# Step zero of a fused attention and mixture-of-experts kernel: weights loaded in halves, VectorE's first work in another order, state copies on ScalarE

## What is computed

```python
q, k, v = xn @ Wq, (xn @ Wk) * DK ** (-0.5), xn @ Wv      # 8 heads, DK = 128, DV = 64
alpha = sigmoid((xn @ Wg + bg) / 16)                       # one per token and head
state = alpha_t * state + k_t[:, None] * v_t[None, :]      # token after token
out_t = q_t @ state
att = (out * sigmoid(xn @ Wog)) @ Wo
```

## Time and profile before

| | us |
|---|---|
| median of 3 runs | 1261.15 (1260.3 to 1261.98) |
| the profiled execution | 1266.82 |
| its span, as the profile shows it | 1265.1 |
| busy in the span: PE | 1237.9 (98%) |
| DVE | 976.6 (77%) |
| ACT | 624.3 (49%) |
| POOL | 487.4 (39%) |

### The profile page before, as it was taken

The page is one execution under the profiler, slowest core; times in us unless marked ns, Lnnn a source line. Parts: engine busy times, 40 slices in busy tenths (PEclk is TensorE's granted clock), DMA queues, the critical chain, the costliest instruction groups (busy, mean ns, idle before and its releaser), DMA issues.

```text
span 1265.1 us, 28662 instructions
## 1 busy us (share of the span) xinstructions
PE 1237.9 (98%) x9910; PEld 1092.2 (86%) x9910; DVE 976.6 (77%) x2343; ACT 624.3 (49%) x1319; POOL 487.4 (39%) x377
## 2 busy tenths in 40 slices
PE   7899999999999999999999999999999999999999
PEld 6788888887888888799899998989989999889987
DVE  6997878889797659878688687786885877868844
ACT  6675756666574544344444444444444444434432
POOL 2110111011001027237467385474574754845620
PEclk9999999999999999999999999999999999999999
DMA  6576534354352322357486575674774765748665
GB/s 241 170 250 200 188 110 156 122 190 158 121 171 60 111 75 84 95 145 186 105 198 165 130 178 136 150 181 106 188 171 121 172 155 137 193 104 191 162 194 183
DMA packets 124920, 194.68 MB, mean 154 GB/s; under 512 B 12016, under 2 KB 98608, under 8 KB 124592
## 3 DMA queue, kind: packets, MB, share of 16 engines
q1 hardware_dynamic: 94384, 147.99, 36.1%
q0 software_dynamic: 30464, 45.83, 19.7%
HBM read 148.62 MB, written 57.74 MB: 163 GB/s over the span
## 4 chain that ended last, share of the span: by engine, by line
PE 76%; DVE 16%; issue 5%; ACT 2%; another core or an unknown queue 0%; DVEq 0%; DMA 0%; ACTq 0%
PE bank L793 21%; PE bank L808 7%; PE bank L905 7%; PE bank L937 7%; PE bank L845 6%; PE bank L825 5%; PE bank L877 3%; PE bank L863 3%; PE bank L866 3%; PE bank L948 3%; PE bank L836 3%; DVE Dt L1506 3%; PE bank L889 2%; PE bank L927 2%; DVE At L1527 2%
## 5 line engine op out<-in xcount | busy, mean ns | idle before, releaser
L635 POOL DMA_INDIRECT acc<-arena,idx_all x128 | 224.3, 1752 | 149.4 <-DMA acc<-res 54.1
L627 POOL DMA_INDIRECT arena<-table,idx_all x132 | 163.6, 1240 | 153.8 <-ACT share L1160 96.5
L793 PE MATMUL bank<-xp,wq 128*128 128x512 f32 x768 | 208.4, 406 | 0.0
L793 PE MATMUL bank<-xp,wk 128*128 128x512 f32 x768 | 202.2, 398 | 0.0
L793 PEld LDWEIGHTS bank<-xp,wk 128*128 128x128 f32 x768 | 138.5, 188 | 29.3 <-DVE wk L1416 0.4
L793 PEld LDWEIGHTS bank<-xp,wq 128*128 128x128 f32 x768 | 136.6, 189 | 25.4 <-issue 0.8
L1506 DVE TENSOR_TENSOR_SCAN Dt<-decay,eye_b 128x512 f32<-128x512 f32 x128 | 157.7, 1233 | 0.0
L845 PE MATMUL bank<-qT,kT 128*128 128x128 f32 x1024 | 136.2, 275 | 1.8 <-DVE At L1527 1.4
L1136 ACT ACTIVATE kT<-bank 128x512 f32<-128x512 f32 x128 | 76.7, 599 | 118.0 <-PE bank L793 102.2
L845 PEld LDWEIGHTS bank<-qT,kT 128*128 128x128 f32 x1024 | 125.2, 192 | 3.3 <-DVE At L1527 1.6
L1136 ACT ACTIVATE qT<-bank 128x512 f32<-128x512 f32 x128 | 76.9, 601 | 85.4 <-PE bank L793 64.7
(11 more groups left out here) (174 smaller groups left out, 2317.1 us busy)
## 6 DMA issues: line engine op xcount, KB each, us to landing
decay<-decay_dram SPq DMA_DIRECT2D x64, 512.0 KB
carry<-decay_dram SPq DMA_DIRECT2D x60, 512.0 KB
arena<-in_L_attn_x_dram SPq DMA_DIRECT2D x16, 512.0 KB, 4.5
table<-arena SPq DMA_DIRECT2D x16, 512.0 KB, 3.2
xT_dram<-arena SPq DMA_DIRECT2D x16, 512.0 KB, 3.0
arena<-in_L_ffn_w_gate_dram SPq DMA_DIRECT2D x64, 128.0 KB
arena<-in_L_ffn_w_up_dram SPq DMA_DIRECT2D x64, 128.0 KB
arena<-in_L_ffn_w_down_dram SPq DMA_DIRECT2D x64, 128.0 KB
```

The source lines that it names most:

```text
L627: pool.indirect_dma_start(out=xg[:, e % 2, j, :], out_offset=None, in_=table[:, :], in_offset=bass.IndirectOffsetOnAxis(ap=idx_all[:, e, j ...
L635: pool.indirect_dma_start(out=acc[:, :], out_offset=bass.IndirectOffsetOnAxis(ap=idx_all[:, e, j:j + 1], axis=0), in_=yb[:, e % 2, j, :], ...
L793: last = mm(to[:, :], w[:, part, k, h * DK:(h + 1) * DK], xp[:, other, k, :], start=(k + i == 0), stop=(k == KD - 1 and i == 2))
```

## The change

Loading. The weights q and k are loaded in halves of four heads each (`q0`, `k0`, `q1`, `k1`), as are their splits. SP's order is x, Wv, gate_w, Wg, q0, k0, the two biases (on a semaphore of their own, `w_bias`), x of block 1 into a buffer of its own (`xt1`, the `addend` tile), og, q1, k1, o. PE waits for gate_w and Wg only.

PE. 24 identity transposes in place of 18 at the start and 6 more between `tokens_back(0, 1)` and `router(0)`; `router(0)` waits for DVE's copies of the tokens and no longer for ACT's; `decays_across(0)` stands behind the first q projection instead of ahead of it.

DVE, ahead of step 0. Splits `v` ahead of the tokens; `gates(0)` ahead of the q and k splits, which are halves; `statistics(1)` ahead of `route_groups(0)`; `route_ranks(0)` and `route_top(0)` ahead of step 0 with the first scans between them; two scans ahead of step 0, not four.

DVE, in step 0. A table of its own for the scans (`first_scans`), with the q1, k1 and o splits in s = 2, 3 and 5; the scan of head 3 of block 1 stands behind all of step 0. No state copies: they are ACT's, `state_first`, at s = 2, 4, 6 and 8 ahead of the high part of `gT`.

ACT, in step 0. `normalise(1)` and the token copies of block 1 (`tokens`) ahead of `keys_weighted(0, 0)`, which moves from ahead of s = 1 into it; the high parts of q1, k1 and o in s = 1, 2 and 3.

SP, in step 0. `norm_io(1)` ahead of `load_decay(0, 3)`.

The end. The third and the fourth pair of batches 0 and 1 are done together, batch after batch.

```diff
-PE_WARM = 18
+PE_WARM = (24, 6)
...
+        xt1 = addend[:, :, :]
...
             def step(c, kind, more=True):
                 first = isinstance(c, int) and c == 0
+                if first:
+                    norm_io(1, more=True)
                 load_decay(c, 3)
...
             tokens_back(0, 0)
             tokens_back(0, 1)
+            for _ in range(PE_WARM[1]):
+                tr(bank[5][:, 0:P], ident[:, :], ident[:, :])
             router(0)
...
                 proj_v(c, kind, 0)
                 if first:
-                    decays_across(0)
                     pe.wait_ge(w_split, 2)
                 proj_qk(c, kind, 0, 0)
+                if first:
+                    decays_across(0)
...
-            out_part(0, (2,))
-            out_part(1, (2,))
             for b in range(B):
-                out_part(b, (KO - 1,))
+                out_part(b, (2, KO - 1) if b < 2 else (KO - 1,))
...
+            def state_first(p):
+                act.wait_ge(u_ps, p + 1)
+                f(state[:, 2 * p:2 * p + 2], bank[6][:, :].rearrange("p (b u v) -> p u b v", b=B, u=2), ACT.Copy)\
+                    .then_inc(state_up, 1)
...
+                    if first and s < 4:
+                        weights_high(("q1", "k1", "o")[s - 1])
+                    if first and s % 2 == 0:
+                        state_first(s // 2 - 1)
                     if s % 2 == 0:
                         outs_high(c, s // 2 - 1)
...
-            tokens_low(0)
             weights_low("v")
-            dve.wait_ge(w_const, 64)
-            weights_low("q")
+            tokens_low(0)
+            dve.wait_ge(w_bias, 32)
             gates(0)
+            weights_low("q0")
+            weights_low("k0")
             decays_products(0)
-            weights_low("k")
+            statistics(1)
             route_groups(0)
-            statistics(1)
-            weights_low("og")
-            scales(1)
...
+            def first_scans(s):
+                for c, h in {1: ((0, 2),), 2: ((0, 3),), 3: ((0, 4),), 4: ((0, 5), (0, 6)), 5: ((0, 7), (1, 0)),
+                             7: ((1, 1), (1, 2)), 9: ((1, 3),)}.get(s, ()):
+                    decay_scan(c, h)
+                if s in (2, 3, 5):
+                    weights_low({2: "q1", 3: "k1", 5: "o"}[s])
...
+            weights_low("og")
+            scales(1)
+            route_ranks(0)
             decay_scan(0, 0)
+            route_top(0)
             decay_scan(0, 1)
-            weights_low("o")
-            decay_scan(0, 2)
-            decay_scan(0, 3)
             step(0, "norm")
```

93 lines of the change are left out of this document (59 added, 34 removed).

## The result

The changed kernel takes **1262.53 us** (median of 22 executions, 1259.92 to 1264.69), the kernel before beside it 1260.72 us (1260.20 to 1262.62, 22 executions): ratio 1.0013, 95% interval 1.0007 to 1.0019. By the forecast's bound of 0.2% this counts as unchanged; by the interval it is a little slower. Forecast were 1257.1 us, in a range that ended at 1261.0 us. The time lies above the range, and it moved in the other direction.

What follows compares the result with a forecast made beforehand. DVE was taken to bound step 0, PE the later steps. Terms -1.45 - 2.05 - 1.64 + 1.2 = -3.94 us, with -0.1 us for the end, took 1261.15 to 1257.1 us; range 1254.9 to 1261.0 us, 8 in 10.

Steps and rivals of the forecast that it cites:

- The start: Ahead of step 0: PE's clock rises early, DVE's copy of the transposed decays starts at 17.5 instead of 18.95 us, -1.45 us.
- Rival 1: At the start: PE's clock does not rise early, decays' copy comes about 20.9 us, total 1260.6 us; chance 0.28.
- The q and k loads: At the start: these loads land behind Wv alone instead of behind the small ones and Wv; costed at nothing.
- the other scans: DVE's step 0 stretch: other scans, o's split, ranks and choice are only reordered; nothing, while others wait for DVE.
- So step 0 costs what stands in DVE's list between those two points: Step 0: DVE's list from the decays' copy to the end of `tokens_low(1)`, 68.43 us, plus the start, sets its length.
- State copies: Step 0: three copies of 0.685 us ahead of `tokens_low(1)` go from DVE to ACT, -2.05 us.
- (a): Step 0, s = 4: DVE waits longer for `gT`'s high part because ACT makes a state copy first, +0.6 us.
- The scan behind: Step 0: the scan of head 3 of block 1 goes behind DVE's stretch, -1.64 us.
- (b): Step 0: DVE waits bare for ACT's square root in s = 6 and the router in s = 8; 0 to 2.8, taken +0.6 us.
- Behind step 0: Entry to step 1: moved scan and later transfers delay DVE against PE; up to 2 us without cover, taken as 0.
- The end: Last output parts and stores: reordered batches change the end by -0.3 to +0.1 us, taken as -0.1 us.
- Rival 2: Step 0: ACT's added copies and high parts make others wait, 1263.2 us; sign: PE waits for ACT over 4 us; chance 0.12.

Runs made afterwards that it cites:

- the second trace: Profiled execution of the unmodified changed kernel, run again on a calmer chip; PE starts step 1 at 86.47 us; that series measured 1261.74 us, ratio 1.0011.
- the short warm-up: Changed kernel with 18 identity transposes at the start and none between token transposes and router: 1263.57 us, ratio 1.0002.
- the new end alone: Kernel before with only the new order of the last output parts: 1261.43 us, ratio 1.0004.
- before with empty instructions: Kernel before with 16 empty instructions ahead of DVE's list, which the build leaves out: ratio 0.9998.
- late loads: Changed kernel with SP's loads of q1, k1 and o issued behind the first two loads of decays: 1263.16 us, ratio 0.9996.
- both edits: Changed kernel with late loads and ACT's square roots of blocks 2 and 3 behind the keys' eviction and update copy: 1262.51 us, ratio 0.9995.
- The combination: Changed kernel with both edits, the old order at the end, and ACT's state copy behind the outputs' high part: first measured 1258.79 us, ratio 0.9984.

## Why the prediction was wrong

The walk of the prediction, step by step:

- **The start, -1.45 us.** Right in mechanism and size: copy at 17.07 us (17.5 forecast; 17.49 us in the second trace). The term was worked out with the router at 1.90 us from 11.7 us on, so with a clock that has risen by then. That was the author's assumption: no row of before shows it that early (3.69 us at 12.37 us). The changed kernel does: nothing but transposes ran from 3.26 us, the eight of 8.89 us take 1.09 us in place of 1.97, and the router 2.00 us from 10.92 us. Rival 1, the late clock, is out. The forecast's premise, that 18 transposes do not bring the rise, was a chance of its trace, though: of the five traces with 18, three (the short warm-up, the new end alone, before with empty instructions) also show the eight in 1.09 to 1.10 us. What holds in all seventeen is the router, 3.69 us with 18 and 2.00 us with 24 and 6. But the gain was not to be had, see the next point.
- **"The q and k loads ... I cost them at nothing", and "the other scans ... only put in another order: nothing". The step that failed first.** The two transfers of decays were never costed, though the reordering puts the first scan behind them at an earlier time. SP has issued the same transfers ahead of the store of the decays, 32 KB, in both kernels (before it issues the second block at 19.45 us, 1.0 us ahead of that store), but the store now comes 1.9 us earlier, while SP is done with issuing the weights and the stores of block 0 3.0 us later (16.00 us against 13.02, the table's store alone taking 4.05 us in place of 0.39). From the store to the loads it is 6.2 us in place of 3.1. Price: 3.1 us of DVE (1.6 us in the second trace). The experiment with late loads gives it back: no wait, and 66.25 us of stretch, 66 forecast.
- **"So step 0 costs what stands in DVE's list between those two points", and PE starting step 1 "right behind" `tokens_low(1)`. Failed too.** With DVE's list shorter PE becomes the bound from s = 6 on: it starts step 1 1.15 us behind `tokens_low(1)` in the changed kernel, in both its traces and with late loads, without a wait. With late loads DVE is done at 83.43 us, as forecast, and PE starts at 84.58. What lies behind s = 6 in DVE's list was counted in full and is worth little. (The stretched instructions in PE's 76.14 us are small beside the slow start: the longest k product of step 0 takes 0.498 us, at 22.06 us, where its weights had waited 0.4 us for DVE's split, against a median of 0.395 us.)
- **State copies, -2.05 us.** Net of wait (a) -1.45 us; undone alone they are worth 1.17 us in DVE's stretch and 0.5 us at PE's step 1.
- **The scan behind, -1.64 us.** Not tested by itself. From DVE's timelines, counting what each scan adds behind the end of the operation ahead of it, twelve scans add 14.30 us to the stretch before and eleven add 12.91 us with late loads: -1.39 us. Both terms were read from durations that overlap their neighbours, and were a little too large; DVE's idle time in the stretch grew by 1.3 us, where (a) and (b) had 1.2 us.
- **Wait (a), +0.6 us.** 1.6 us in s = 4, where 1.7 was forecast. A second wait of 1.0 us stands in s = 8 behind another state copy, in the profiled execution too (at 90.24 us); it lies behind `tokens_low(1)` and no term had it. The forecast's list of DVE's waits before left out a row of 0.7 us (for ACT's copy of the tokens): 4.5 us in all and not 3.8.
- **Wait (b), 0 to 2.8 us, 0.6 taken.** Looked for on the wrong engine. DVE waits 0.3 us for the square root, as a bare hand-over. But the square root waits for DVE 2.37 us, and what stands behind it on ACT are the copies that PE needs. I had asked who is queued behind the waiting instruction on DVE, and not on ACT. PE waits 2.11 us for it. Another 1.4 us, in s = 3, stand behind the other square root, but not because that one waits: ACT loads a table for it, and the keys' eviction is behind both.

```profile
47.44 1.28 ACT L1088 ACT_TABLE_LOAD   x1
...
49.48 0.66 PE L860 MATMUL bank<-ident,kT 128*128 128x128 f32 x4 [1.38 <-ACT kT L1165]
```

Taken out of the way the wait moved to the next place (2.1 us ahead of L732), so its price is small; late loads alone reach 84.58 us, both edits 83.96 us: 0.6 us, of which 0.2 us is the start (copy of the decays at 17.18 and 16.94 us). The bare router in s = 8 cost DVE 0.98 us in the profiled execution, 0.27 us with a held clock.
- **The clock in s = 6: no term.** 1.56 us in the profiled execution. I had treated the clock as a matter of the start only.
- **Behind step 0, 0 (up to 2 us).** As an effect of late transfers right: step 1 has its 0.3 us and no more. (With late loads DVE does wait for the load of block 4, 0.6 us, and 1.3 us with both edits, and PE's step 1 is not longer for it.) But 0.88 us came from the place of the instructions in DVE's list, which no term and no rival had. "From step 1 on the lists of all engines are as before" is the sentence that failed.
- **The end, -0.1 us.** +0.2 us on average. The last pair's part stops PE 0.17 us (forecast 0.1), and the last sum ends 0.13 to 0.17 us later, while the first store, 0.21 us earlier, brings nothing.

The sum for the profiled execution: step 1 at 89.08 us in place of the forecast 83.5 us, 5.6 us; steps 1 to 3, 0.9 us; end, 0.3 us; together 6.8 us. 1257.1 + 6.8 = 1263.9 us, measured 1263.15 us. For the median take the second trace, whose clock held: 86.47 - 83.5 = 3.0, and 0.9 and 0.3, gives 1261.3 us. The executions with a mean clock of 1.000 took 1259.6 to 1261.25 us, so this sum is some 1 us high; 0.4 us of it is the base (1261.15 us of three executions, 1260.72 us of the 22 beside the changed kernel), the rest is open. Executions with a fallen clock take up to 4.8 us more than the fastest.

Rival 2 gave the time, 1263.2 us, by luck. Its sign, PE waits for ACT of over 4 us in step 0, decides nothing: they are 9.5 us, but the kernel before already has 5.6 us. New are 3.9 us, and 2.3 us in the second trace. Its mechanism is another one: not the work that ACT got, but in the main what ACT itself waits for, ahead of copies that PE needs. Shown are the wait for the decays by an experiment, the fall of the clock as the difference between two pairs of traces, PE as the bound from s = 6 on from the traces, and the place in DVE's list by two experiments (three memsets that shift it by 2 make the steps 0.24 to 0.31 us longer, 32 that shift it by 31 take 0.24 to 0.25 us off them). Why the clock falls behind a gap of 1.8 or 2.1 us in one execution and not in the next is open.

## What to carry to other kernels

When an engine is the bound and you give it less to do, follow for each of its early instructions who hands it its data, transfers with their round trip included, and see which of them was late only by grace of the old pace. When a list gets shorter, ask which engine is the next bound and from where on: only what is saved ahead of that place counts. In front of each wait in a list that another engine feeds, read what stands behind it: two queues that wait for each other in turn cost the third engine (here ACT waited 2.37 us for DVE, and PE 2.11 us for ACT). Let a store and load back of a few KB that others wait for go ahead of MBs that nobody needs yet (here 32 KB ahead of 1.5 MB: 1.9 us from store to load in place of 4.7 and 6.2). And compare the lengths of the untouched steps between two traces: a shift of a list by two entries cost 0.2 to 0.3 us in each of three.

The combination that came out of this, ratio 0.9971 to 0.9984 over five series on three chips, beats both kernels, the one before by 0.2 to 0.3%. Of the 2.6 us by which PE starts step 1 earlier than in the changed kernel with a held clock (86.47 to 83.89 us), 1.9 us came with the order of SP's loads, which costs no work at all. In the medians of the single edits that gain is not clear of the scatter.
